# Experts: the multiplication by the gate moves from GpSimd to VectorE

## The reference

```python
gate_logits = xf @ Wg + bg                      # 8 experts
top_w, top_i = jax.lax.top_k(gate_logits, 2)
top_w = jax.nn.softmax(top_w, axis=-1)
w_dense = jnp.sum(jax.nn.one_hot(top_i, E) * top_w[..., None], axis=1)
for e in range(E):
    h = jax.nn.gelu(xf @ W1[e] + b1[e], approximate=False)    # 256 -> 1024
    out = out + w_dense[:, e:e + 1] * (h @ W2[e] + b2[e])     # 1024 -> 256
```

## Time and profile before

| | us |
|---|---|
| median of 3 executions | 1247.88 |
| lowest and highest | 1243.93, 1252.08 |
| the profiled execution | 1247.95 |
| its span, first to last instruction | 1246.1 |
| TensorE busy in the span | 1096.8 |
| VectorE busy | 759.0 |
| ScalarE busy | 743.1 |
| GpSimd busy | 731.0 |
| last tiles evicted at | 1224.50 and 1229.74 |

### The profile page before, as it was taken

The page is one execution under the profiler, slowest core; times in us unless marked ns, Lnnn a source line. Parts: engine busy times, 40 slices in busy tenths (PEclk is TensorE's granted clock), DMA queues, the critical chain, the costliest instruction groups (busy, mean ns, idle before and its releaser), DMA issues. The chain is left out here.

```text
span 1246.1 us, 37906 instructions
## 1 busy us (share of the span) xinstructions
PE 1096.8 (88%) x12025; PEld 953.0 (76%) x12026; DVE 759.0 (61%) x2691; ACT 743.1 (60%) x1771; POOL 731.0 (59%) x786
## 2 busy tenths in 40 slices
PE   4998888999999879972299999999999999998994
PEld 2666678999999868862178888888888888887783
DVE  7887787998989849976144444444444444443341
ACT  3556577898989847753155555555555555555541
POOL 7323255676666616777446666666666666665454
PEclk9999898999999989976599999999999999999998
DMA  7889788788788559997212322323323232323122
GB/s 180 235 253 272 226 225 206 195 205 195 193 202 202 161 187 352 370 311 246 91 15 48 52 49 47 52 43 52 49 49 51 43 52 48 52 48 46 33 41 26
DMA packets 150570, 168.43 MB, mean 135 GB/s; under 512 B 15694, under 2 KB 141694, under 8 KB 150086
## 3 DMA queue, kind: packets, MB, share of 16 engines
q1 hardware_dynamic: 109270, 123.59, 34.8%
q0 software_dynamic: 21984, 31.18, 14.3%
q10 hardware_dynamic: 19232, 12.64, 4.7%
HBM read 107.52 MB, written 64.70 MB: 138 GB/s over the span
## 5 line engine op out<-in xcount | busy, mean ns | idle before, releaser
L1698 ACT ACTIVATE e_g_hi<-e_ps_h,keep_b 128x256 f16<-128x256 f32 x392 | 203.0, 518 | 247.5 <-PE e_ps_h L1601 247.4
L1764 DVE TENSOR_TENSOR e_g_lo<-e_gf,e_g_hi 128x256 f16<-128x256 f32 x424 | 184.2, 434 | 161.4 <-ACT e_gf L1698 139.6
L1635 PE MATMUL e_ps_y<-w2s,e_g_hi 128*128 x1696 | 282.1, 273 | 0.0
L1601 PE MATMUL e_ps_h<-e_xt,w1s 128*128 128x256 f16 x2352 | 269.4, 275 | 4.8 <-PEq L1593 4.3
L1601 PEld LDWEIGHTS e_ps_h<-e_xt,w1s 128*128 x2352 | 224.4, 98 | 43.8 <-issue 10.3
L977 POOL TENSOR_TENSOR b_p<-b_s,b_p 128x392 f16<-128x392 f32 x196 | 178.9, 934 | 96.3 <-DVE b_p L864 82.7
L1635 PE MATMUL e_ps_y<-w2s,e_g_lo 128*128 x848 | 231.8, 273 | 0.0
L1553 POOL DMA_INDIRECT out<-e_y,e_xg x106 | 176.3, 1663 | 84.0 <-POOLq L1548 41.1
L1698 ACT ACTIVATE e_gf<-e_ps_h,keep_b 128x256 f32<-128x256 f32 x392 | 205.5, 524 | 0.0
L1635 PEld LDWEIGHTS e_ps_y<-w2s,e_g_hi 128*128 128x128 f16 x1696 | 164.3, 98 | 18.6
L923 ACT ACTIVATE b_s<-b_s,b_neg_max 128x196 f32<-128x196 f32 x392 | 158.9, 458 | 0.3 <-DVE b_neg_max L845 0.2
(11 more groups left out here) (175 smaller groups left out, 1666.2 us busy)
## 6 DMA issues: line engine op xcount, KB each, us to landing
h_v<-v_rows SPq DMA_DIRECT2D x196, 99.5 KB
e_xg<-slots SPq DMA_DIRECT2D x49, 273.0 KB, 2.7
a_w_in<-in_w SPq DMA_DIRECT2D x16, 512.0 KB, 4.8
c_w_in<-in_w SPq DMA_DIRECT2D x16, 512.0 KB, 9.3
v_rows<-h_v_sb SPq DMA_DIRECT2D x14, 455.0 KB, 7.1
a_x<-in_x SPq DMA_DIRECT2D x14, 448.0 KB, 6.6
qk_hi<-h_o_hi SPq DMA_DIRECT2D x14, 448.0 KB, 4.8
qk_lo<-h_o_lo SPq DMA_DIRECT2D x14, 448.0 KB, 5.7
```

The source lines that it names most:

```text
L1601: mm = pe.matmul(ps_h[:, hc % 4, 0:ST], w1s[:, bass.ds(e, 1), w, a:a + 128].rearrange("p a n -> p (a n)"), xt[:, s, :, 2 * p + k, :], star ...
L1635: mm = pe.matmul(ps_y[:, s, h * C:(h + 1) * C], g[:, s, hc, h * 128:(h + 1) * 128], w2s[:, bass.ds(experts[h], 1), w, a:a + C].rearrange(" ...
L1698: last = act.activation(dst, ps_h[:, hc % 4, 0:ST], ACT.Gelu, bias=b1_sb[:, bass.ds(e * HC + hc, 1)], scale=1.0 / WSCALE)
L1764: dve.tensor_tensor(g_lo[:, s, hc, :], gf[:, hc % 4, :], g_hi[:, s, hc, :], ALU.subtract).then_inc(gs_ok, 1)
```

## The change

GpSimd no longer multiplies. `take_y` on VectorE evicts to `y_f` as before, waits for its own result (`y_out`), for the gate (`gate_ok`) and for a free `y_sb` (`y_free`), multiplies the two halves by their gates into `y_sb`, and only then gives `yf_ok`. On GpSimd `weigh` gives `gate_ok` and no longer waits for it, and `send` gives `xg_free` and `y_free` when the transfers of the tile before have landed, and issues its own. The scratch `ex` gets a buffer for each of the four tiles.

```diff
@@ weigh (the three steps before it change only ex[:, :] to ex[:, j, :])
-                    pool.tensor_tensor(gate[:, j, :], ex[:, :], invert[:, :], ALU.pow).then_inc(gate_ok, 1)
-                    pool.wait_ge(gate_ok, 1)
-                    pool.sem_inc(gate_ok, -1)
+                    pool.tensor_tensor(gate[:, j, :], ex[:, j, :], invert[:, :], ALU.pow).then_inc(gate_ok, 1)
@@ send
                     if n is not None:
                         pool.wait_ge(y_done, 32 * n)
                         pool.sem_inc(xg_free, 1)
-                    for h in range(2):
-                        last = pool.tensor_scalar(y_sb[:, s, h, :], y_f[:, s, h, :], gate[:, j, h:h + 1], None, ALU.mult)
-                    last.then_inc(y_out, 1)
-                    pool.wait_ge(y_out, 1)
-                    pool.sem_inc(y_out, -1)
-                    pool.sem_inc(y_free, 1)
+                        pool.sem_inc(y_free, 1)
@@ take_y
                     dve.wait_ge(y_ok, 1)
                     dve.sem_inc(y_ok, -1)
-                    if not begins:
-                        dve.wait_ge(y_free, 1)
-                        dve.sem_inc(y_free, -1)
...
-                    dve.scalar_tensor_tensor(y_f[:, s], ps_y[:, s, :].rearrange("p (h c) -> p h c", h=2),
-                                             1.0 / WSCALE, b2_sb[:, bass.ds(e, 1), :].to_broadcast([128, 2, C]),
-                                             ALU.mult, ALU.add).then_inc(yf_ok, 1)
+                    else:
+                        last = dve.scalar_tensor_tensor(
+                            y_f[:, s], ps_y[:, s, :].rearrange("p (h c) -> p h c", h=2), 1.0 / WSCALE,
+                            b2_sb[:, bass.ds(e, 1), :].to_broadcast([128, 2, C]), ALU.mult, ALU.add)
+                    last.then_inc(y_out, 1)
+                    dve.wait_ge(y_out, 1)
+                    dve.sem_inc(y_out, -1)
+                    dve.wait_ge(gate_ok, 1)
+                    dve.sem_inc(gate_ok, -1)
+                    if not begins:
+                        dve.wait_ge(y_free, 1)
+                        dve.sem_inc(y_free, -1)
+                    for h in range(2):
+                        last = dve.tensor_scalar(y_sb[:, s, h, :], y_f[:, s, h, :], gate[:, j % U, h:h + 1], None, ALU.mult)
+                    last.then_inc(yf_ok, 1)
```

More of the change, by code:

```diff
@@ L1448, in stage_e @@
         gap = sb("e_gap", [128, U, 2, 2], F32)
-        ex = sb("e_ex", [128, 2], F32)
+        ex = sb("e_ex", [128, U, 2], F32)
         gate = sb("e_gate", [128, U, 2], F32)
@@ L1522, in weigh @@
                     pool.sem_inc(gap_ok, -1)
-                    pool.tensor_tensor(ex[:, :], gap[:, j, :, 0], gap[:, j, :, 1], ALU.add).then_inc(sum_ok, 1)
+                    pool.tensor_tensor(ex[:, j, :], gap[:, j, :, 0], gap[:, j, :, 1], ALU.add).then_inc(sum_ok, 1)
                     pool.wait_ge(sum_ok, 1)
                     pool.sem_inc(sum_ok, -1)
-                    pool.tensor_tensor(ex[:, :], euler[:, :], ex[:, :], ALU.pow).then_inc(pow_ok, 1)
+                    pool.tensor_tensor(ex[:, j, :], euler[:, :], ex[:, j, :], ALU.pow).then_inc(pow_ok, 1)
                     pool.wait_ge(pow_ok, 1)
                     pool.sem_inc(pow_ok, -1)
-                    pool.tensor_scalar(ex[:, :], ex[:, :], 1.0, None, ALU.add).then_inc(sum_ok, 1)
+                    pool.tensor_scalar(ex[:, j, :], ex[:, j, :], 1.0, None, ALU.add).then_inc(sum_ok, 1)
                     pool.wait_ge(sum_ok, 1)
                     pool.sem_inc(sum_ok, -1)
-                    pool.tensor_tensor(gate[:, j, :], ex[:, :], invert[:, :], ALU.pow).then_inc(gate_ok, 1)
-                    pool.wait_ge(gate_ok, 1)
-                    pool.sem_inc(gate_ok, -1)
+                    pool.tensor_tensor(gate[:, j, :], ex[:, j, :], invert[:, :], ALU.pow).then_inc(gate_ok, 1)
                 def send(j, n, apart=False):
@@ L1557, in _ @@
                 pool.memset(euler[:, :], math.e)
-                pool.memset(invert[:, :], -1.0).then_inc(gate_ok, 1)
-                pool.wait_ge(gate_ok, 1)
-                pool.sem_inc(gate_ok, -1)
+                pool.memset(invert[:, :], -1.0).then_inc(sum_ok, 1)
+                pool.wait_ge(sum_ok, 1)
+                pool.sem_inc(sum_ok, -1)
                 weigh(0)
@@ L1785, in take_y @@
                                 b2_sb[:, bass.ds(experts[h], 1), :].rearrange("p a c -> p (a c)"), ALU.mult, ALU.add)
-                        last.then_inc(yf_ok, 1)
-                        return
-                    dve.scalar_tensor_tensor(y_f[:, s], ps_y[:, s, :].rearrange("p (h c) -> p h c", h=2),
-                                             1.0 / WSCALE, b2_sb[:, bass.ds(e, 1), :].to_broadcast([128, 2, C]),
-                                             ALU.mult, ALU.add).then_inc(yf_ok, 1)
+                    else:
[13 more added lines that the diff above has]
+                    last.then_inc(yf_ok, 1)
                 half_tables()
```

## The result

The changed kernel takes 1276.99 us, the median of 4 runs (1273.28 to 1279.98), against 1249.45 for the kernel before on the same chip (4 runs, 1243.93 to 1252.08). The ratio is 1.0225, interval 1.0178 to 1.0272: **28 us slower**, where I had forecast 1246.7 and a range up to 1254. The profiled execution took 1273.28, its span 1271.5.

What follows compares the result with a forecast made beforehand. TensorE was taken to bound mid-stage and GpSimd's chain the end. From 1247.95 us, -2.9 at the end and +1.7 in the middle gave 1246.7 us, range 1242.5 to 1254.

Steps and rivals of the forecast that it cites:

- the last bullet of the sum: Row loads: xg_free given about 1.1 us later, the load wanted about 16 us later, so costed at nothing.
- The waits before the multiplications: VectorE's take_y: three waits ahead of the multiplications cost 0.15 + 2 x 0.10 = 0.35 us.
- The multiplications: VectorE's take_y: two of 128x256 float32 cost 0.65 us, 0.32 from start to start, bounds 0.38 and 0.65.
- The subtraction's slip: VectorE behind take_y: first subtraction slips 0.28 us, 0.05 beyond the free 0.23; TensorE loses 1.7 us over 34 tiles.
- VectorE held up by GpSimd: Rival, 12%: GpSimd's gate arithmetic holds take_y's multiplications up to 0.71 us, TensorE waits, 26 us, 1271 us.
- The end: Last two tiles: tile 52's first scatter starts at 1233.95 against 1236.82, -2.9 us.
- The signs I named: Wrong if multiplications exceed 0.5, idle before them exceeds 0.7, or TensorE's mid-stage share falls by over 1%.

Runs made afterwards that it cites:

- e4: e1 with the constant 0.5 in place of the gate in VectorE's two multiplications; 1262.92 us in a single run.
- e5: e1 with one multiplication of 128x512 by the first gate in place of two of 128x256; 1235.28 us in a single run on the faster chip.
- e1: The changed kernel with xg_free and y_free given before yf_ok is waited for; 1266.9 us, ratio 0.9945 to the kernel before.
- e2: The kernel before, multiplications still on GpSimd, with xg_free given before the wait for yf_ok; 1269.3 us, ratio 0.9961.
- e7: The changed kernel with an extra pair of multiplications per tile on VectorE, into a scratch, ahead of the true one; 1300.23 us, ratio 1.041.
- e6: e1 with an extra pair of multiplications per tile on VectorE, into a scratch, ahead of the true one; 1258.15 us, ratio 1.0072.
- e8: The changed kernel measured again with no edit, on another chip; 1275.7 us, ratio 1.0204 to the kernel before.

## Why the prediction was wrong

**The step that failed** is the last bullet of the sum: "That load is wanted one and a half periods later, about 16 us, so I cost it at nothing." I had seen that `xg_free` moves and by how much (about 1.1, measured 1.00 after the eviction's start, 0.90 after the up pass's), and then counted the tiles wrongly, with no row behind the count. `send(n)` releases the buffer of tile n - 1, since what has landed are that tile's transfers. With four buffers that buffer belongs to tile n + 3. TensorE's order is `up(n + 1)`, `turn(n + 2)`, `down(n)`, `up(n + 2)`, `turn(n + 3)`: `take_y(n)` runs beside `up(n + 2)`, and the rows are wanted directly behind it. From the load's issue to the transposes it is 2.96 us (910.56 - 907.60), from the eviction's start 4.76, and not 16: under half a period. The trace of before held all of it: SyncE's row at 907.60, a median of 2.7 from issue to landing, the transposes at 910.56. I had not set these beside each other, nor the eight waits for rows that it already had, 8.3 us in all (a mean period of 11.087, where I wrote 10.95). The term was worth 0.76 us a tile and 31.8 in all, and I put it at 0.

- **The waits before the multiplications**: 0.38, forecast 0.35. Right.
- **The multiplications**: 350 ns each and 0.27 from start to start, forecast 0.32. From the first one's start to the subtraction behind the pair it is 0.53 (943.92 to 944.45), forecast 0.65, in the middle between 0.38 and the 0.65 that I took as likeliest. Rows 9 misled me there: L309's 408 ns fit two scalars of 60 ns each on top of a constant's 291, and not a slower rate. By the Trainium skill (VectorE: DVE Perf Modes, "The perf-mode tier table") `tensor_scalar` in float32 from SBUF runs at two elements a cycle, and takes 1227 ns for 2048 elements, which by my estimate is 0.60 each with what is fixed in it. The slopes in e4 and e5, without the fixed part, agree with it: 0.50 and 0.53 ns an element.
- **The subtraction's slip**: the first one ends 0.19 before chunk 4 in e1 and in the changed kernel, where 0.14 is needed, so TensorE loses nothing. Forecast +1.7 us; e1's period is no longer than e2's (11.020 and 11.027), so about 0. The subtraction starts 1.60 after an eviction that is 0.10 earlier, so it slips by 0.19, forecast 0.28: the pair is 0.12 shorter and the waits 0.03 longer.
- **VectorE held up by GpSimd** (12%, 1271): its time is the nearest to what came, and its mechanism did not happen. The multiplications start 1.63 after GpSimd's last gate step has ended (943.92 against 941.59 + 0.70), and none of the 106 takes over 354 ns. That its time came near is luck.
- **The end**: the last scatters are released as worked out. From the last eviction to the end it takes 13.46 us instead of 16.37: -2.9, as forecast. The unexplained idle time before the last scatter stayed (GpSimd of the changed kernel, last four transfers). The last one starts at 1266.275, 0.45 after the one ahead of it has landed (1265.824):

```profile
1255.41 1.54 POOL L1546 DMA_INDIRECT out<-e_y,e_xg  x1 [6.97 <-POOLq L1538]
1257.26 1.54 POOL L1546 DMA_INDIRECT out<-e_y,e_xg  x1 [0.30 <-issue]
1261.98 1.54 POOL L1546 DMA_INDIRECT out<-e_y,e_xg  x1 [3.19 <-DMA out<-e_y,e_xg]
1266.28 1.54 POOL L1546 DMA_INDIRECT out<-e_y,e_xg  x1 [2.75 <-issue]
```

- **The signs I named**: TensorE's share in mid-stage fell by 7%, which I had named as the sign of being wrong. The other two, multiplications over 0.5 or a wait over 0.7, did not show, and that pointed away from `take_y`.

## What to carry to other kernels

When an edit moves the point where an engine gives a semaphore, list everything that stands behind it in program order, and for each buffer that is released there write down which tile takes it next and which instruction waits for that tile; then read the distance from the trace of before, release to landing to first use, and not from the number of buffers. A busy share of 99.8% on TensorE says that nothing is late, and not by how much: here the loads had 0.15 us left at most. A release that does not depend on a result belongs ahead of the wait for it: that order alone is worth 0.4%, and it is what makes the move a gain (0.55% in all) instead of a loss of 2.2%.

## What the runs showed of the hardware

- A per-partition scalar costs a float32 `tensor_scalar` on VectorE a fixed 60 ns (350 against 291 for 128x256) and leaves 0.53 ns an element. Two scalars are in line with that: L309 has two, 112x256, and takes 408 ns.
- A row load of 273 KB takes 2.66 us from issue to landing in the changed kernel's tile and 2.68 in the one of before, near the medians of 2.8 and 2.7, and TensorE starts 0.14 after a landing that it waits for.
- Two late inputs of one engine overlap: a stop of 0.58 in the up pass cost nothing where the rows were later still (e7), and 16 to 20 us where they were early (e6).
- The idle time before the last scatter is in all ten traces, 2.55 us (e2) to 2.77 (e8), and each time the scatter starts 0.45 after the one ahead of it has landed (1240.58 and 1241.03 before the change), though the code has no wait between the two. The second scatters of tiles 50 and 51 start 0.30 after the end of the first. What makes the last one wait stays open; no run was made for it.
